# Second attention of a two-layer vision tower: head groups in strips of 32 rows, routed rows normalized on ScalarE, and the two best experts found by maxima

## The reference, cut to what matters

```python
q = _layernorm((x @ Wq.T).reshape(b, t, 8, 16), q_gamma, q_beta)     # per head
k = _layernorm((x @ Wk.T).reshape(b, t, 8, 16), k_gamma, k_beta)
v = (x @ Wv.T).reshape(b, t, 8, 16)
scores = jnp.einsum('bqhs,bkhs->bhqk', q, k) * scale
scores = jnp.where(cols > rows, -jnp.inf, scores)
attn = jax.nn.softmax(scores, axis=-1)
h = h + jnp.einsum('bhqk,bkhs->bqhs', attn, v).reshape(b, t, 128) @ Wo.T + bo
x = _layernorm(h)                                                     # no gains
logits = x @ Wg + bg                                                  # 8 experts
w, idx = jax.lax.top_k(logits, 2)
w = jax.nn.softmax(w, axis=-1)      # then the experts' products, weighted by w
```

## Time and profile before

| | us |
|---|---|
| median of 3 runs | 1944.51 (1939.29 to 1944.73) |
| the profiled execution, its own time | 1945.98 |
| its span in the profile | 1944.2 |
| TensorE matmul busy | 1670.3 (86%) |
| VectorE busy | 1219.6 (63%) |
| ScalarE busy | 1064.8 (55%) |
| GpSimd busy | 1138.5 (59%) |

### The profile page before, as it was taken

How to read it: one execution, slowest core, us unless ns; L and a number is a source line. 1 busy time by engine, 2 the same in 40 slices (tenths; PEclk the granted TensorE clock), 3 DMA queues, 4 the chain that set the end, 5 groups by cost and what they waited for, 6 DMA issues and landing times. The chain is left out here.

```text
span 1944.2 us, 44781 instructions
## 1 busy us (share of the span) xinstructions
PE 1670.3 (86%) x13211; PEld 1258.8 (65%) x13212; DVE 1219.6 (63%) x4791; ACT 1064.8 (55%) x2510; POOL 1138.5 (59%) x1040
## 2 busy tenths in 40 slices
PE   4999999984479763899999999999983999999995
PEld 2665666663457542476776766766762898988985
DVE  2899899983732003689999999999974222222221
ACT  2666666652445442567666667667651555555553
POOL 2455554432068873136566666666565777777776
PEclk8999999995579886899999999999995999999998
DMA  8989899932023433112112112111113676767764
GB/s 199 239 210 220 214 217 230 229 77 59 0 57 67 67 50 80 41 31 55 49 47 55 49 46 56 49 46 52 40 44 85 119 139 126 135 128 127 136 130 78
DMA packets 272309, 198.11 MB, mean 102 GB/s; under 512 B 27118, under 2 KB 252688, under 8 KB 272144
## 3 DMA queue, kind: packets, MB, share of 16 engines
q1 hardware_dynamic: 221072, 160.12, 33.0%
q0 software_dynamic: 49984, 35.38, 13.2%
q10 hardware_dynamic: 1088, 0.53, 0.1%
HBM read 143.33 MB, written 52.40 MB: 101 GB/s over the span
## 5 line engine op out<-in xcount | busy, mean ns | idle before, releaser
L2321 POOL DMA_INDIRECT out_dram<-r_yw,r_idx x212 | 328.6, 1550 | 116.2 <-issue 67.3
L2210 POOL DMA_INDIRECT rows_scratch<-routed_row,slot_u x256 | 252.0, 984 | 205.0 <-DVE slot_u L2161 141.8
L1883 ACT ACTIVATE a_probsT<-a_p_sc 98x392 f32<-98x392 f32 x384 | 170.5, 498 | 154.9 <-PE a_p_sc L1664 90.5
L2387 ACT ACTIVATE r_hT<-r_p_up,r_b1T 128x256 f32<-128x256 f32 x424 | 191.6, 474 | 114.6 <-PE r_p_up L2362 110.9
L2349 PEld LDWEIGHTS r_p_y<-w_all,r_hT 128*128 128x128 f32 x1696 | 224.0, 193 | 11.4 <-issue 0.3
L2349 PE MATMUL r_p_y<-w_all,r_hT 128*128 x1696 | 224.8, 276 | 0.0
L2362 PE MATMUL r_p_up<-r_xgT,r_w1e 128*128 128x256 f32 x848 | 221.6, 385 | 0.6 <-ACT r_xgT L2392 0.6
L448 PE MATMUL p_embed<-pix,w_pix 96*128 96x392 f32 x512 | 210.3, 518 | 3.5 <-ACT pix L567 3.5
L2403 DVE TENSOR_TENSOR r_yb<-r_p_y,b_all 128x256 f32<-128x256 f32 x106 | 45.0, 424 | 190.0 <-PE r_p_y L2349 182.1
L717 POOL TENSOR_SCALAR vare<-mv 98x4 f32<-98x4 f32 x64 | 29.9, 468 | 219.6 <-DVE mv L702 200.3
L1981 DVE TENSOR_REDUCE a_negmax<-a_p_max 98x2 bf16<-98x392 f32 x256 | 131.9, 555 | 41.1 <-PE a_p_max L1631 40.9
(11 more groups left out here) (365 smaller groups left out, 4051.3 us busy)
## 6 DMA issues: line engine op xcount, KB each, us to landing
img<-in_x_dram SPq DMA_DIRECT2D x192, 196.0 KB, 4.4
img<-in_x_dram SPq DMA_DIRECT2D x192, 189.0 KB, 4.5
r_w1e<-in_L_ffn_W_dram SPq DMA_DIRECT2D x106, 256.0 KB
r_xg<-rows_scratch SPq DMA_DIRECT2D x106, 130.0 KB, 2.4
xn_scratch<-xn SPq DMA_DIRECT2D x32, 196.0 KB
h_scratch<-h SPq DMA_DIRECT2D x32, 196.0 KB
h<-h_scratch SPq DMA_DIRECT2D x32, 196.0 KB
h3b<-h_scratch SPq DMA_DIRECT2D x32, 196.0 KB
```

Of the source, the lines that this page charges most:

```text
L1883: act.activation(probsT[:, u % 2, i, :], p_sc[i % 2][:, 0:2 * PAIR], ACT.Exp).then_inc(exped, 1)
L2210: pool.indirect_dma_start(rows_dram, bass.IndirectOffsetOnAxis(ap=slot_u[:, u % ROWS, c, t:t + 1], axis=0), row[:, u % ROWS, c, t, :], Non ...
L2321: pool.indirect_dma_start(acc_dram, bass.IndirectOffsetOnAxis(ap=idx[:, (k - 3) % 4, t:t + 1], axis=0), yw[:, (k - 3) % 4, t, :], None, co ...
L2387: act.activation(hT[:, (k - 1) % 2, f, :], p_up[f][:, 0:G], ACT.Silu, bias=b1T[:, bass.ds(e * FC + f, 1)]).then_inc(act_h, 1)
```

## The change

It has three parts. First, the array is used in strips of 32 rows (`STRIP`), each with two heads, so `q_var` has two variants in place of four (`LIVE = 2`), and places 0 and 1 of a group lie in strips 0 and 2, places 2 and 3 in strips 1 and 3. `score_products` and `max_products` become generators that `in_turn` runs alternately: half of the scores, half of the maxima products, and again. A score product of 392 columns is written as two of 196. Second, DVE no longer writes the normalized rows; ACT does, as x * rstd4 + shift4, in which POOL makes `shift4` = -mean * rstd4 with two more operations. ACT's copy for the second expert moves behind the exponentials of places 2 and 3. Third, the two best experts are found by a maximum, a comparison with it, a product with a priority that takes the first of equals (`prio`), its maximum and a second comparison; then the same over the logits with the best one pushed down. These 13 operations stand between others (`choose`), each `later` waiting for the one before.

```diff
-        LIVE = HEADS // 2
+        LIVE = 2
+        STRIP = 32
...
                 def places(i):
                     group, at = divmod(i, 4)
-                    half, two = divmod(ORDER[at], 2)
-                    return (0, None, 1)[group], slice(64 * half, 64 * half + 64), 2 * two, 2 * ORDER[at]
+                    strip = ORDER[at]
+                    return (0, None, 1)[group], slice(STRIP * strip, STRIP * (strip + 1)), 0, 2 * strip
...
-                    for both in zip(*spans):
+                    for k, both in enumerate(zip(*spans)):
...
+                        if 2 * k + 2 == len(spans[0]):
+                            yield
...
                     for x in range(2):
+                        if x:
+                            yield
...
-                            elif x == 0:
+                            else:
                                 o = m * PAIR
-                                pe.matmul(p_sc[p][:, 0:2 * PAIR], kT[rows, s4, o:o + TILE],
-                                          q_var[rows, s4, var:var + 2, o:o + PAIR], start=True, stop=False,
+                                pe.matmul(p_sc[p][:, x * PAIR:(x + 1) * PAIR], kT[rows, s4, o:o + TILE],
+                                          q_var[rows, s4, var + x, o:o + PAIR], start=(x == 0), stop=False,
                                           skip_group_check=True)
...
                 def scores_and_max(i, skew, j, later):
-                    if on[skew]:
-                        score_products(i, n - skew)
-                    if on[later]:
-                        max_products(j, n - later)
+                    in_turn(*([score_products(i, n - skew)] if on[skew] else []),
+                            *([max_products(j, n - later)] if on[later] else []))
...
-                    done(act, ln4, N["ln4"], u)
+                    done(act, rstd4_r, 4, u)
                     scatter_done(act, u - ROWS)
-                    act.copy(row[:, u % ROWS, 1, :, 0:D], row[:, u % ROWS, 0, :, 0:D]).then_inc(row2_ready, 1)
+                    done(act, xn4_turned, 1, u - ROWS)
+                    for t in range(TPU):
+                        last = act.activation(row[:, u % ROWS, 0, t, 0:D], h4[:, u % 2, t, :], ACT.Identity,
+                                              bias=shift4[:, u % 2, t:t + 1], scale=rstd4[:, u % 2, t:t + 1])
+                    last.then_inc(row_ready, 1)
...
                 exps(2, 4, 4)
+                if on[6]:
+                    u = n - 6
+                    done(act, row_ready, 2, u, 1)
+                    act.copy(row[:, u % ROWS, 1, :, 0:D], row[:, u % ROWS, 0, :, 0:D]).then_inc(row_ready, 1)
                 exps(4, 6, 4)
...
+                def first_of_best(c, logits):
+                    yield from t_st.later(dve.tensor_reduce(best[:, c, :], logits, X, ALU.max))
+                    yield from t_st.later(dve.tensor_tensor(tmp8[:], logits, bcast(best[:, c, :], EXPERTS), ALU.is_equal))
+                    yield from t_st.later(dve.tensor_tensor(tmp8[:], tmp8[:], prio[:], ALU.mult))
+                    yield from t_st.later(dve.tensor_reduce(lead[:], tmp8[:], X, ALU.max))
+                    yield from t_st.later(dve.tensor_tensor(oh[:, c], tmp8[:], bcast(lead[:], EXPERTS), ALU.is_equal))
...
-                rows((0, 1, 2, 3))
...
+                    pool.tensor_scalar(minus4[:], mv4[:, u % 2, :, 0], -1.0, None, ALU.mult).then_inc(rstd4_r, 1)
+                    inverse_root(rstd4[:, u % 2, :], vare4[:, u % 2, :], mv4[:, u % 2, :, 1], 1.0, rstd4_r, 4 * u + 1)
+                    wait(pool, rstd4_r, 4 * u + 3)
+                    pool.tensor_tensor(shift4[:, u % 2, :], minus4[:], rstd4[:, u % 2, :], ALU.mult
+                                       ).then_inc(rstd4_r, 1)
```

98 lines of the change are left out of this document (43 added, 55 removed).

## The result

The changed kernel takes 1938.52 us (median of 20 runs, 1932.81 to 1945.01), the kernel before, on the same chip, 1945.05 (20 runs, 1939.29 to 1948.36): ratio 0.9972, 95% interval 0.9963 to 0.9981. It is faster by 0.3%, 6.5 us, where 29.5 were forecast. The profiled span is 1939.0 us against 1944.2.

A forecast was written before the change was run, and what follows sets the result against it. TensorE and VectorE were taken to hand the turn to each other in a ring. 1.05 us a turn over 25 turns (26 us) plus 3.5 us for seven others gave 1944.5 - 29.7 = 1915 us, range 1896 to 1937.

The forecast's parts named there:

- The step of the pipeline: TensorE's scores and maxima overlap fully on strips: 1.01 to 0.84 us a step, six steps, 1.0 us a turn.
- overlap fails: Rival: strips share a port or issue in turn, steps stay at 1.01 us, 1934 us in all; chance 0.15.
- the estimate worked out from the 3.07x of the Trainium skill: Strips at 77% of full speed: 0.65 us of scores would be 0.85, and the overlap would gain nothing.
- VectorE relieved by 1.2 to 2.8 us: VectorE's work a turn: 4.13 us removed, less 13 added small operations and a possible wait; 1.8 us taken.
- its busy share: Sign of being right: VectorE waits for masks two or three times a turn, its busy share below 88%.
- ScalarE's rows: Four normalizations added on ScalarE behind `vals` of the last tile: 1.0 us of work, 0.15 us charged to the turn.
- TensorE waiting over 0.5 us for `routed_row`: Sign of being wrong: TensorE waits more than 0.5 us for the routed rows.
- no difference: Rival: ScalarE's rows come late by 1 us instead of 0.15 and eat the gain, 1942 us; chance 0.06.
- (c): From the reduction of places 2 and 3 to the turning of `qkn`, 7.91 us, untouched; TensorE waits longer for `qkn`.
- TensorE alone: Rival: only TensorE's own work sets the turn, 19.2 us, gain 1.6 a turn, 1900 us in all; chance 0.12.
- The sum of a turn: In the steady attention a turn loses 1.03 to 1.14 us, 1.05 taken, 26 us over 25 turns.
- The other seven turns: Turns lacking early or late pipeline stages were given half the gain each, 3.5 us in all.

The follow-up runs named there:

- rows_top2_plain: Changed kernel without strips (halves of 64 rows), with ordinary DMAs for the indirect scatters and only padding in the routed stage: 1926.65 us, 0.991 of the kernel before.
- changed_third: The changed kernel without any edit, run again on a chip that raises semaphores late: 2067.4 us, 1.0513 of the kernel before beside it.
- strips_top2: Changed kernel with the routed rows normalized on VectorE again, strips and maxima kept: 2013.72 us, 1.0201 of the kernel before beside it.
- top2_only: The kernel before with only the two best experts found by maxima: 1974.75 us, 1.0007 of the kernel before beside it.
- strips_serial: Changed kernel with all score products of a step written before its maxima products: 2069.68 us, 1.0507 of the kernel before beside it.

## Why the prediction was wrong, by its own steps

- *The step of the pipeline, 1.01 to 0.84 us by full overlap*: right in size, wrong in number. 0.84 exactly, but in five steps of six; in the fifth of the table the maxima wait for VectorE's reduction, and it stays at 1.00. A step without any maxima products takes 0.84 too (1418.32 to the score maxima at 1419.16, after). The rival "overlap fails" falls, and so does, for this shape, the estimate worked out from the 3.07x of the Trainium skill (TensorE: Matmul & The Clock Gate, Part 3), by which no step would have shortened.
- *VectorE relieved by 1.2 to 2.8 us, 1.8 taken*: 2.1 measured. TensorE's waits for it in two steps (1.98 and 2.11 against 1.74 and 1.73 in rows_top2_plain) are gone. VectorE waits twice a turn, and its busy share is 86%, as forecast.
- *ScalarE's rows, 1.0 us of work, 0.15 us charged*: this is the mis-sized term of the steady sum. The work is 1.55 us, and TensorE waits 0.59 us. The nearest rows were copies of a whole tile (0.67 for 98x512) and of a PSUM tile (0.28), and the true price, 0.39 a piece, is above both; most of the error of 0.55 falls on TensorE, since ScalarE is busy without a gap ahead of it. The text gave "TensorE waiting over 0.5 us for `routed_row`" as a sign of being wrong. The rival "no difference" named this wait; it was right on the mechanism, at about half its size. That this wait bounds the turn is argued: no run took it away without putting work back on VectorE, which then came late itself.
- *(c), the chain to `qkn`, 7.91 us as the next late thing*: not so. TensorE waits for `qkn` 0.25 us a turn (6.0 us in 24), not longer than before. With ordinary DMAs that wait is gone, and the turn goes from 20.17 to 19.93. What is left is TensorE with its wait for rows: 19.93 - 0.60 = 19.3 is an estimate of a turn without it, close to the 19.2 of the rival "TensorE alone"; no run reached it.
- *The sum of a turn*: 1.05 forecast, 0.67 to 0.70 measured, 16.7 us over 25 turns instead of 26.
- *The other seven turns, half a gain each, 3.5 us*: this failed, and it is the larger error. They cost 10.6 us, so this term is off by 14 us, the 25 steady turns by 9.3. The forecast looked at the ends as shorter copies of the steady turn, and not at what a faster TensorE leaves idle there, nor at the clock. For the first end it is shown that the clock at half costs 4 to 5 us (101 us, 96 with fillers, on two kinds of chip). For the drain, 8.9 of the 10.6 us, it is not shown by an edit: its length follows the time at 1.2 GHz, 59 us against 39, but a kernel without fillers escaped it too, and what sets it off stays open. Fillers with the scatters as they are, on a chip like the recorded one, were not run.

-16.7 + 10.6 and +0.7 of the rest make the -5.4 us.

Open: on chips that raise semaphores late, why the strips turn a loss of 0.2 us a turn (before) into one of 4.4. It takes the indirect scatters: without them, on such a chip, the loss is nil. The clock is one part: changed_third's mean of 0.85 means 1.2 GHz for three tenths of the stretch, by estimate up to 0.15 x 24.5 = 3.7 us a turn. It is not all: strips_top2 keeps a whole clock (1.00, 900 to 1360 us) and has turns of 22.37 us, where top2_only on the same chip has 21.21. TensorE also idles more in the steady stretch there (41 us in the 25 turns of changed_third, 18 in after). That the shorter steps leave less slack for a late raise is argued, not shown.

## What to carry to other kernels

When work moves to an engine whose own idle share is large, look at the gap directly ahead of the place where it goes: with none, most of the error of its price lands on who waits for it. Count each occurrence of a step before multiplying a gain, and price the ends of a pipeline by themselves: an engine made faster idles there, and TensorE's clock, at half for longer, can take back more than the ends could have gained. A gain of 0.3% on one chip can be a loss of 5% on another of the same kind, so the pair is measured on more than one.

## What the runs showed of the hardware

- On four of the five chips of the experiments, semaphores were raised late, in one case 7.8 us after the instruction that makes the raise, where the trace of before has 15 ns. In the steady attention it comes with GpSimd's indirect scatters; with ordinary DMAs of the same rows, on such a chip, no raise there is late.
- Score products in float32 on two strips and maxima products in bf16 on the two others ran at once: two score records and all four maxima records start before 1100.34, within 0.24 us, and the maxima add nothing to the step. In strips_serial the maxima, written behind all scores, start 0.03 us behind the first: products on free strips start ahead of earlier ones whose strips are taken.
- Four normalizations of 98x128 on ScalarE, with scale and bias from SBUF, take 0.39 us each; 0.18 us operations of VectorE take 1.0 to 1.4 beside a working GpSimd.
